# A probability buffer for each tile, one run of value products for two tiles, and `a_v(1)` behind the first expert's first products

## The reference

```
# layer 0, modulated by nine vectors m = silu(mod) @ w_ada + b_ada of the batch
h = ln(x)*(1+sc)+sh;  qkv of h, rolled by -64; windows of 128 tokens, 16 heads of 16
attn = softmax(q k / 4);  o = attn v, rolled back;        x = x + (o @ w_so + b_so)*g
h = ln(x)*(1+sc)+sh;  q = h @ w_q, k and v of the 77 context rows
top 16 of the 77 scores, softmax of them, o = attn v;     x = x + (o @ w_co + b_co)*g
h = ln(x)*(1+sc)+sh;                                      x = x + swiglu(h)*g
# layer 1, experts
nx = ln(x)*gamma+beta;  evidence = softmax((nx Wq)(ctx Wk) / 16) (ctx Wv)
combined = [nx, evidence, cond]
router = softmax(combined @ router_W + router_b)
routed = sum over 3 experts of (silu(combined @ e_w1 + e_b1) @ e_w2 + e_b2) * router
x + sigmoid(silu(combined @ gate_w1 + ..) @ gate_w2 + ..) * (routed @ out_w + out_b)
```

## Time and profile before

| | |
|---|---|
| three runs | 1445.49, 1446.76, 1450.96 us; median 1446.76 |
| the profiled execution, first to last instruction | 1447.1 us (a time around the span isn't recorded) |
| TensorE, VectorE, ScalarE, POOL busy | 1413.0, 1061.7, 837.8, 437.8 us |
| DMA | 34.99 MB, 24 GB/s in the mean, most of it in the first tenth |

### The profile page before, as it was taken

One profiled execution on the slowest core, in us unless ns is written; L12 is line 12 of the kernel. 1 busy time (PEld: TensorE's weight loads), 2 busy tenths in 40 slices (PEclk: granted clock), 3 DMA queues, 4 the chain that ended last, 5 costly groups with the idle time before them and its releaser, 6 DMA issues.

```text
span 1447.1 us, 30246 instructions
## 1 busy us (share of the span) xinstructions
PE 1413.0 (98%) x9777; PEld 1195.1 (83%) x9777; DVE 1061.7 (73%) x4754; ACT 837.8 (58%) x2555; POOL 437.8 (30%) x599
## 2 busy tenths in 40 slices
PE   7999999999999999999999999999999999999997
PEld 5778788888888888888888788888888878887886
DVE  3585869688796878879696777959688786968642
ACT  3464475757566384755757466574757547574433
POOL 1314132333325232332335232233334313232302
PEclk9999999999999999999999999999999999999999
DMA  7520000010000000010010000000010000000000
GB/s 244 196 73 2 1 1 25 1 34 9 19 31 15 1 2 25 2 34 2 21 36 2 15 2 16 11 15 20 8 43 8 16 2 1 9 2 8 1 2 14
DMA packets 27342, 34.99 MB, mean 24 GB/s; under 512 B 3325, under 2 KB 22449, under 8 KB 26930
## 3 DMA queue, kind: packets, MB, share of 16 engines
q1 hardware_dynamic: 27185, 33.07, 7.1%
HBM read 28.83 MB, written 4.22 MB: 23 GB/s over the span
## 4 chain that ended last, share of the span: by engine, by line
PE 83%; DVE 12%; issue 2%; ACT 1%; SPq 0%; POOL 0%; DMA 0%; DVEq 0%; ACTq 0%; POOLq 0%
PE bank L965 13%; PE bank L920 12%; PE bank L989 10%; PE bank L972 7%; PE bank L791 6%; PE bank L929 6%; PE bank L777 4%; PE bank L852 4%; PE bank L840 4%; PE bank L904 4%; DVE knocked L2224 3%; PE bank L830 2%; PE bank L748 2%; PE bank L762 2%; PE bank L812 1%
## 5 line engine op out<-in xcount | busy, mean ns | idle before, releaser
L920 PE MATMUL bank<-hB,Wm 128*128 128x256 f32 x1024 | 242.3, 383 | 2.2 <-ACT hB L1366 2.2
L920 PEld LDWEIGHTS bank<-hB,Wm 128*128 128x128 f32 x1024 | 190.6, 190 | 33.4 <-issue 7.0
L965 PE MATMUL bank<-nxT,W1nx 128*128 128x256 f32 x896 | 212.1, 382 | 0.0
L1405 ACT ACTIVATE prob<-bank,rmax 128x128 f32<-128x128 f32 x512 | 180.3, 432 | 28.3 <-DVE rmax L2151 28.3
L1762 POOL TENSOR_TENSOR scores<-scores,M 128x308 f32<-128x308 f32 x128 | 94.5, 738 | 320.1 <-DVE knocked L2224 317.7
L1412 ACT ACTIVATE probT<-bank 128x512 f32<-128x512 f32 (+1 forms) x256 | 140.3, 617 | 83.8 <-PE bank L904 76.8
L989 PE MATMUL bank<-W2p,gT 128*128 128x256 f32 x768 | 183.2, 381 | 3.0 <-DVE acc L2303 1.9
L965 PEld LDWEIGHTS bank<-nxT,W1nx 128*128 128x128 f32 x896 | 166.1, 191 | 23.1 <-issue 2.8
L989 PEld LDWEIGHTS bank<-W2p,gT 128*128 128x128 f32 x768 | 141.2, 190 | 23.8 <-issue 2.8
L1450 ACT ACTIVATE tbs<-bank,b1half 128x256 f32<-128x256 f32 x128 | 60.7, 474 | 143.1 <-PE bank L920 102.2
L1466 ACT ACTIVATE tbs<-bank,betaH 128x256 f32<-128x256 f32 x224 | 95.6, 489 | 82.7 <-PE bank L972 82.7
(11 more groups left out here) (238 smaller groups left out, 2772.4 us busy)
## 6 DMA issues: line engine op xcount, KB each, us to landing
Wm_g<-in_L_xcond_w_m_dram SPq DMA_DIRECT2D x4, 1024.0 KB, 5.4
W1ev<-in_L_xcond_e_w_dram SPq DMA_DIRECT2D x6, 512.0 KB, 7.2
x<-in_x_dram SPq DMA_DIRECT2D x16, 128.0 KB, 2.6
x<-in_x_dram SPq DMA_DIRECT2D x32, 64.0 KB, 2.3
Wm<-in_L_xcond_w_m_dram SPq DMA_DIRECT2D x1, 2048.0 KB, 9.3
out_dram<-acc SPq DMA_DIRECT2D x16, 128.0 KB, 1.7
out_dram<-acc SPq DMA_DIRECT2D x32, 64.0 KB, 2.0
batch_rows<-row_store SPq DMA_DIRECT2D x4, 384.0 KB, 3.9
```

The lines of the kernel that those rows point to most:

```text
L920: m = pe.matmul(bank_of(name)[:, half * UT:(half + 1) * UT], Wm1[:, k, c:c + P], hB[:, k, :], start=(k == 0), stop=(k == CB - 1))
L965: pe.matmul(bank_of(name)[:, n * UT:(n + 1) * UT], W1nx[:, k, c0 + n * P:c0 + (n + 1) * P], nxT[:, k, :], start=(n == 0 and k == 0), stop= ...
L1405: m = act.activation(prob[:, s, i, :], psum[s][:, i * P:(i + 1) * P], ACT.Exp, bias=rmax[:, t, s * HPS + i:s * HPS + i + 1], accum_out=rsu ...
```

## The change

`probT` gets one buffer for each tile. To make room, three small tiles of the prologue (`out_row`, `split_b`, `onehot`) are laid into other tiles that are not yet in use, or made smaller. On TensorE `a_cross_values(0)` moves down to stand directly ahead of `a_cross_values(1)`, `a_values(0)` moves down to stand directly ahead of `a_values(1)`, and `a_v(1)` moves behind the first products of expert 0. The same is done with the cross values in `last_cross`. The prologue's order is kept. In the diff two lines that only rename `out_row[:, :]` to `out_row` are left out.

```diff
@@ -224,7 +224,7 @@
         prob = sb("prob", [P, SLOTS, HPS, P])
         scores = sb("scores", [P, TILES * H * LC])
         S = scores[:, :].rearrange("p (t h c) -> p t h c", t=TILES, h=H)
-        probT = sb("probT", [P, SLOTS, HPS, P])
+        probT = sb("probT", [P, TILES, SLOTS, HPS, P])
         rsum = sb("rsum", [P, TILES, H])
         rinv = sb("rinv", [P, TILES, H])
         oT, q2T = hA, qT
@@ -272,10 +272,10 @@
         W1an = W1ev
         gate_rows = [gs[0:NB, 0, :], gs[0:NB, 1, :], nxT[0:NB, 0, :]]
         rows = Vp[0:NB, 0:len(BIAS) * C].rearrange("b (n c) -> b n c", n=len(BIAS))
-        out_row = sb("out_row", [1, C])
+        out_row = bias_term[0:1, 0, :]
         split = tbs[0:NB, :, :].rearrange("b i (n c) -> b (i n) c", c=C)
-        split_b = sb("split_b", [NB, 4, C], BF16)
-        onehot = sb("onehot", [NB, NB, P])
+        split_b = sb("split_b", [1, len(SHARED), C], BF16)
+        onehot = bias_sum[0:NB, :, :].rearrange("b t c -> b (t c)").rearrange("b (n q) -> b n q", q=P)
         condT = sb("condT", [P, CB, NB])
         bv4 = sb("bv4", [P, 2, CB, NB])
         siluT = sb("siluT", [P, CB, NB])
@@ -850,7 +850,7 @@
                     for e in range(PAR):
                         for s in range(SLOTS):
                             m = pe.matmul(bank_of(name)[32 * s:32 * s + 32, f * UT + t * P:f * UT + (t + 1) * P],
-                                          v[:, f * SLOTS + s, 32 * e:32 * e + 32], probT[0:np_, s, f * PAR + e, :],
+                                          v[:, f * SLOTS + s, 32 * e:32 * e + 32], probT[0:np_, t, s, f * PAR + e, :],
                                           start=(e == 0), stop=(e == PAR - 1))
                 if t == TILES - 1:
                     m.then_inc(full[JOB[name][0]], 1)
@@ -1180,13 +1180,10 @@
                 if r == 1:
                     pe.wait_ge(readB, batch * 5 + 5)
                 a_turn_picked(0, 3, c)
-                a_v(1, a)
                 b_proto_scores(b)
                 b_first_nx("h00", 0, b)
                 b_first_nx("h01", 2 * P, b)
-                if r == 0:
-                    pe.wait_ge(values_read, batch + 1)
-                a_cross_values(0, c)
+                a_v(1, a)
                 b_turn_weights(b)
                 if r == 3:
                     pe.wait_ge(readA, batch * 2 + 2)
@@ -1201,6 +1198,9 @@
                 b_first_evidence("h10", RH, b)
                 a_turn_inverses("r2", "xv", c)
                 b_router(b)
+                if r == 0:
+                    pe.wait_ge(values_read, batch + 1)
+                a_cross_values(0, c)
                 a_cross_values(1, c)
                 a_scores(0, range(SLOTS), a)
                 b_first_evidence("h11", RH + 2 * P, b)
@@ -1215,7 +1215,6 @@
                 a_turn_probs(0, 3, a)
                 b_second(0, (2, 3), b)
                 a_scores(1, range(SLOTS), a)
-                a_values(0, a)
                 b_second(1, (0, 1), b)
                 b_first_nx("h21", 2 * RH + 2 * P, b)
                 a_turn_probs(1, 0, a)
@@ -1226,6 +1225,7 @@
                 b_first_evidence("h20", 2 * RH, b)
                 b_first_evidence("h21", 2 * RH + 2 * P, b)
                 a_turn_inverses("r1", "pv", a)
+                a_values(0, a)
                 a_values(1, a)
                 b_first_nx("hg", 3 * RH, b)
                 if r == 3:
@@ -1409,7 +1409,7 @@
             def a_copy_turned(t, s, u, kind, np_=P):
                 name = f"{kind}{t}{s}"
                 wait_full(act, name, u)
-                act.activation(probT[0:np_, s], psum[s][0:np_, :].rearrange("p (i q) -> p i q", i=HPS), ACT.Copy)\
+                act.activation(probT[0:np_, t, s], psum[s][0:np_, :].rearrange("p (i q) -> p i q", i=HPS), ACT.Copy)\
                    .then_inc(drained[s], 1)
 
             def a_copy_inverses(name, values, u):
```

More of the change, by code:

```diff
@@ L395, in bass_pixart_experts @@
         gated_loads = [(Wso_g[:, :, :], blocks(w_so)), (Wco_g[:, :, :], blocks(w_co))]
-        folded_loads = [every_batch(rrow[:, :], router_b), (out_row[:, :], rank1(out_b)), (rows[0:1, BIAS.index("g2"), :], rank1(gate_b2)),
+        folded_loads = [every_batch(rrow[:, :], router_b), (out_row, rank1(out_b)), (rows[0:1, BIAS.index("g2"), :], rank1(gate_b2)),
                         (Rw[:, :, :], blocks(router_w)), (outw, blocks(out_w)), (wk_sb, blocks(wk1)), (wq_sb, blocks(wq1))]
@@ L2046, in expert_bias @@
                     r = rows[0:1, BIAS.index("e0") + e, :]
-                    i = dve.scalar_tensor_tensor(r, bk[0:1, (e % 2) * C:(e % 2 + 1) * C], 4.0, out_row[:, :], ALU.mult, ALU.add)
+                    i = dve.scalar_tensor_tensor(r, bk[0:1, (e % 2) * C:(e % 2 + 1) * C], 4.0, out_row, ALU.mult, ALU.add)
                     if e != es[-1]:
```

## The result

The changed kernel takes 1472.74 us (median of 4 runs, 1470.38 to 1475.49), the one before 1446.8 on the same chip: ratio 1.0164, interval 1.0146 to 1.0182. It is 1.6% slower by that ratio, 1.8% by the two medians; 1471 was forecast.

A forecast was written before the change was run, and what follows sets the result against it. VectorE's list up to the cross inverses and the softmax chain in the second tile's self-attention were taken as the bounds. 14 x (0.87 + 0.87) = 24.4 us on 1447.1 gave 1471 us, range 1459 to 1476.

The forecast's parts named there:

- What bounds: VectorE's unbroken list up to the cross inverses; in tile 1's self-attention TensorE's filler just matches the softmax chain, 9.14 us.
- Buffers: A `probT` for each tile and the prologue's borrowed rows add no instruction: cost 0.
- One run for two: 16 more products in the same run cost 0.87 us; the run that goes away gives back 1.01 us.
- dearer rival: The second tile costs a whole run at both places: 28.3 us in all, 1475 us; chance 0.05.
- Cross values: Tile 0's, moved behind cross inverses and router: gain 0 ahead, cost 0.87 us a step behind; lower bound -0.47.
- the 1.34 us: TensorE time freed ahead of the cross inverses: 0.9 lost waiting at `b_turn_weights`, 0.4 at the inverses.
- Self values: Tile 0's, moved behind the `r1` inverses: 1.01 us becomes a wait at `a_turn_probs(1, ...)`; cost 0.87 us a step.
- Last cross step: Only the cross values move there; between -0.47 and +0.87 us, taken as 0.
- Sum: 14 x (0.87 + 0.87) = 24.4 us on 1447.1: 1471.5, forecast as 1471 us.
- Faster: Rival: TensorE's own list decides at both places, so saved run boundaries give 8.5 us, 1438 us; chance 0.05.
- point of decision: The faster rival decides from where VectorE's list is 1.3 us shorter.
- One loop only: Rival: one place is exposed, the other gains or costs nothing: 1452, 1457 or 1459 us; chance 0.08.

The follow-up runs named there:

- e5: The changed kernel plus idle identity products on TensorE in both holes of each full step; ratio 1.0172 to the kernel before.
- e6: The changed kernel with the scaling of the next queries moved from VectorE to ScalarE; ratio 1.0127 to the kernel before.
- e4: As e3, with the third expert's evidence products moved into the hole and between the transposes of tile 1; ratio 1.0007 to the kernel before.
- e3: The changed kernel with the cross values and a_v(1) put back, so only the self values are joined; ratio 1.0096 to the kernel before.
- e1: The changed kernel's buffers and borrowed rows with TensorE's old order put back; ratio 0.9990 to the kernel before.
- e2: The changed kernel with the self values put back, so only the cross values are joined; ratio 1.0083 to the kernel before.
- e9: As e7, plus the third expert's evidence products inside the softmax of tile 1 (half of them where r = 0); ratio 1.0029 to the kernel before.
- e8: As e6, with the cross values apart again and the third expert's evidence products inside tile 1's softmax; ratio 0.9971 to the kernel before.
- e7: As e6, with VectorE normalising `pw` one top-k round earlier; ratio 1.0120 to the kernel before.

## Why the prediction was right

- **What bounds.** Right, and shown from both sides: more work on TensorE at these places costs nothing (e5), less on VectorE brings the inverses 0.51 us forward in each step (e6), another filler in the softmax loop turns a loss of 0.87 us a step into a gain of 0.07 (e4 against e3). A TensorE that is 97 or 98% busy proved nothing. The Trainium skill's page Perfetto Trace Analysis, section Identifying the Most-Contended Engine, says that busy time of the products is a bad measure of how close TensorE is to its limit; the trace agrees, since 14 waits of 0.34 us told more than 98%. One reading was too wide: that VectorE never stops was read from one step. In the four steps with r = 1 it waits for TensorE's products for the context (L748), more than 3 us in three pauses. They end ahead of the place that the change touches, and the way to the inverses is the same there too (52.53 and 52.54 us in the first of these steps, before and after).
- **Buffers**, 0: measured 0.0 (e1).
- **One run for two**, +0.87: the joined blocks take 1.88, so 1.88 - 1.01 = 0.87. The dearer rival is out.
- **Cross values**, +0.87 a step: e2 gives 0.88. Where the 1.34 us would go was only partly right. 0.9 was to be lost at `pw` and 0.4 at the cross inverses; in this step it is 0.85 at `pw`, 0.28 ahead of the turned picks of tile 1, and 0.05 more for POOL than before at the inverses. In 11 other steps a part of it goes to L942, up to 0.5 for ScalarE, which the prediction had not listed. All of them are inside the same hole, so the time is the same.
- **Self values**, +0.87 a step: e3 gives 0.87. The wait is at `a_turn_probs(1, ...)` as stated, two thirds of it already at the first slot (0.69 and 0.28).
- **Last cross step**, 0: -0.29 (44.25 to 43.09 us ahead of the inverses, 23.38 to 24.25 behind). At the same mean clock of 0.96 it takes 67.3 to 67.4 with the cross values joined (after, e5, e6) and 66.9 to 67.6 with them apart (before, e1, e3, e4), so that no change can be told from 0.
- **Sum**, 24.4: measured 24.1 in the 14 full steps, 23.8 with `last_cross`. From median to median it is 25.9; the other 2.1 lie outside the steps, and the profiled execution shows 1.6 of them in the last experts (below). The prediction took 0.3 us off its sum because no time outside the span was recorded; the execution after took 1474.44 us for a span of 1472.7, so 1.7 lie outside. In the kernel before it is as much (1445.51 us for a span of 1443.7, beside e9), so they cancel, and the 0.3 should have stayed.
- **Faster**: the rival's mechanism exists, each run that is saved gives 0.14 us by the blocks, and e4 gains as much where the loop is filled. Its point of decision was not reached: with VectorE's list 0.6 us shorter, and not 1.3, joining the cross values still loses 0.47 a step (e9 against e8). **One loop only** is out by e2 and e3.

What stays open: `last_cross` differs by 0.7 us among kernels with the same lists and the same mean clock in it. `a_v(1)` was moved in no run by itself. And it wasn't tried why VectorE's list is 0.15 us longer in e7 than in e6.

## What to carry to other kernels

Moving work off a stretch where another engine decides gains nothing there, and the work has to be done again where this engine decides: look for the place that the work leaves (is there a filler?) before looking at what the new place saves. A chain that keeps its length to 0.02 us at places hundreds of us apart, and short waits that come once a step, mark such stretches better than a busy share. When a batch of small runs is to be joined, put other ready work into the hole in the same edit.

## What the runs showed of the hardware

**The end of the program at two clocks.** The columns of these windows are us, busy us of PE, PEld, DVE, ACT and POOL (instructions), granted clock, DMA share and GB/s. The last experts of the kernel before, from 30 us behind their start:

```profile
1408.42:1428.42 20.00, 18.00 (x85) 15.26 (x84) 6.33 (x15) 6.54 (x18) 7.59 (x6) 1.00 0.05 14
```

and after:

```profile
1432.34:1452.34 20.00, 18.01 (x78) 15.01 (x77) 5.78 (x15) 6.52 (x18) 7.56 (x6) 0.91 0.05 14
```

`last_experts` takes 68.7 us before, with a granted clock of 1.00 in this window (2.4 GHz throughout), and 70.3 after, with 0.91 (1.2 GHz for a part of it); TensorE was busy for 18.0 of 20 us both times. The order of the change doesn't settle it: e5 has it and takes 68.7, as before and e1; e2 takes 70.3, e3 and e4 72.0. In the measure of fifteen steps it has no part.

`last_cross` shows the same. From its start to its inverses, in e6 and in e7, whose TensorE lists are the same:

```profile
1328.67:1371.75 43.08, 39.44 (x220) 33.47 (x219) 38.16 (x230) 20.61 (x48) 8.95 (x14) 0.96 0.03 7
```

```profile
1328.83:1373.07 44.24, 40.89 (x220) 35.04 (x219) 38.24 (x230) 20.64 (x48) 8.94 (x14) 0.92 0.03 7
```

With a mean granted clock of 0.96 it is 43.1 us with the cross values joined (after, e5, e6) and 43.6 to 44.3 with them apart (before, e1, e3, e4); with 0.92 it is 43.9 to 44.2 (e2, e7, e9) and 44.8 (e8). TensorE was busy for 39.4 and 40.9 us of the two stretches shown. The clock was 1.2 GHz for a part of the stretch in every kernel.

**VectorE beside POOL.** All 56 weighings before, from shortest to longest (ns), and POOL in a step with r = 0:

```profile
L2168 DVE TENSOR_TENSOR prob<-prob,rinv x56: 691/693/1018, 196.5 to 1294.0; 128x512 f32<-128x512 f32 x56
...
441.35 7.77 POOL L1810 TENSOR_TENSOR Wm_g<-Wm_g,batch_rows 128x256 f32<-128x256 f32 x8
```

The weighing takes 0.69 us by the median; the last three of this step (from 444.56 on, 1.02, 1.01 and 1.01 us) lie within POOL's 7.77 us. So it is in all three steps with r = 0: the 12 weighings beside this POOL operation take 0.90 to 1.02 us, and the 44 others 0.69, of which 33 run beside other operations of POOL (11 for 0.60 us beside its copies of one input, L1783). The Trainium skill's page GPSIMD Engine Reference, section Specifications, names contention of the two engines for VectorE's operations with two inputs in SBUF, which these are; the trace agrees for POOL's operation of two inputs, though no run here separated the two. In these steps the softmax loop is longer, 9.01 us to the last transposes against 8.68.
